# Linear attention with a ternary feed-forward layer: a matmul stage moved beside the next group's, and hi parts ahead of lo parts

## The reference

```python
def feature_map(x, orf):
    proj = x @ orf.T / d_k ** 0.25
    norm = jnp.sum(x * x, axis=-1, keepdims=True) / (2.0 * math.sqrt(d_k))
    return (jnp.exp(proj - norm) + EPS) / math.sqrt(m)
q = feature_map(split(x @ Wq.T + bq), orf)
k = feature_map(split(x @ Wk.T + bk), orf)
v = split(x @ Wv.T + bv)
kv = jnp.einsum('nlm,nld->nmd', k, v)
ksum = jnp.sum(k, axis=1)
buf = jnp.concatenate([kv, ksum[..., None]], axis=-1)
out = jnp.einsum('nlm,nmd->nld', q, buf)
out = out[..., :-1] / out[..., -1:]
# heads joined again, then
x = _layernorm(x + (out @ Wo.T + bo))
x = _layernorm(x + x @ (ternary(weight) * scale).T)
```

## Time and profile before

| | |
|---|---|
| time, median of 3 runs | 1310.24 us (1308.63 to 1312.22) |
| the profiled execution | 1310.11 us, span 1308.2 us |
| mean granted TensorE clock | 0.998 |
| busy: TensorE, weight loads, VectorE | 98%, 74%, 72% of the span |
| busy: ScalarE, GpSimd | 54%, 39% |
| TensorE in the chain that ended last | 83% |
| HBM | 39.13 MB read, 16.78 MB written |

### The profile page before, as it was taken

One profiled execution on the slowest core, in us unless ns is written; L12 is line 12 of the kernel. 1 busy time (PEld: TensorE's weight loads), 2 busy tenths in 40 slices (PEclk: granted clock), 3 DMA queues, 4 the chain that ended last, 5 costly groups with the idle time before them and its releaser, 6 DMA issues.

```text
span 1308.2 us, 25147 instructions
## 1 busy us (share of the span) xinstructions
PE 1279.2 (98%) x8570; PEld 965.2 (74%) x8570; DVE 946.1 (72%) x1791; ACT 701.9 (54%) x1403; POOL 511.1 (39%) x1005
## 2 busy tenths in 40 slices
PE   9999999999999999999999999999999999999886
PEld 8767787777877678776787768876788767886655
DVE  7599765886668775787657786577765787657866
ACT  5556535564355743657336663367544665346634
POOL 1325433345333443325424344334453334433343
PEclk9999999999999999999999999999999999999999
DMA  7557314763145721567215762257602675036611
GB/s 237 146 129 217 94 46 111 177 176 91 57 123 145 207 67 55 131 152 193 61 57 129 182 165 67 61 136 200 161 33 70 154 202 140 33 95 140 165 33 65
DMA packets 94015, 160.37 MB, mean 123 GB/s; under 512 B 31168, under 2 KB 47680, under 8 KB 93376
## 3 DMA queue, kind: packets, MB, share of 16 engines
q1 hardware_dynamic: 67856, 139.78, 41.5%
q10 hardware_dynamic: 9648, 16.85, 3.4%
q0 software_dynamic: 16384, 2.13, 1.2%
HBM read 39.13 MB, written 16.78 MB: 43 GB/s over the span
## 4 chain that ended last, share of the span: by engine, by line
PE 83%; DVE 5%; ACT 3%; SPq 3%; DMA 3%; issue 2%; POOL 1%; ACTq 0%; POOLq 0%; DVEq 0%
PE ps L927 27%; PE ps L964 24%; PE ps L1025 8%; PE ps L950 4%; PE ps L996 4%; PE ps L952 4%; PE ps L951 4%; PE ps L983 4%; PE ps L1051 2%; DMA rows<-in_x_t 1%; SPq L519 1%; ACT features L671 1%; SPq L508 1%; DMA rows<-in_Wk_t 1%; DMA stacks<-norm_rows 1%
## 5 line engine op out<-in xcount | busy, mean ns | idle before, releaser
L671 ACT ACTIVATE features<-ps 128x512 f32<-128x512 f32 x512 | 278.3, 601 | 257.3 <-PE ps L927 197.5
L574 POOL DMA_DIRECT2D stacks<-norm_rows x512 | 251.4, 499 | 397.4 <-DVE norm_rows L852 173.7
L553 POOL TENSOR_SCALAR stats<-stats 128x1 f32<-128x1 f32 x128 | 36.4, 284 | 317.9 <-DVE stats L780 317.9
L927 PE MATMUL ps<-Wo_hi,stacks 128*128 128x512 f32 x448 | 150.5, 402 | 0.0
L645 ACT ACTIVATE values_then_attention<-ps 128x512 f32<-128x512 f32 x64 | 38.2, 597 | 197.3 <-PE ps L952 194.0
L793 DVE TENSOR_TENSOR den<-den,features 128x512 f32<-128x512 f32 x192 | 132.3, 689 | 13.8 <-ACT features L671 0.4
L927 PE MATMUL ps<-orf_key_a,stacks 128*128 128x256 f32 x512 | 131.7, 289 | 1.1 <-DMA stacks<-norm_rows 1.1
L1025 PE MATMUL ps<-features,kv_ksum 128*32 128x512 f32 x1024 | 123.1, 598 | 5.9 <-ACT features L671 4.6
L927 PE MATMUL ps<-orf_key_b,stacks 68*128 68x256 f32 x512 | 128.5, 283 | 0.0
L829 DVE SCALAR_TENSOR_TENSOR unit_lo<-ps,cols,unit_hi 128x512 fp32r<-128x512 f32 x128 | 94.3, 736 | 35.0 <-ACT squares L655 35.0
L927 PEld LDWEIGHTS ps<-orf_key_a,stacks 128*128 128x128 f32 x512 | 97.1, 190 | 26.9 <-issue 23.0
(11 more groups left out here) (136 smaller groups left out, 2726.6 us busy)
## 6 DMA issues: line engine op xcount, KB each, us to landing
stacks<-unit_hi SPq DMA_DIRECT2D x384, 128.0 KB, 2.4
stacks<-unit_lo SPq DMA_DIRECT2D x256, 128.0 KB, 3.2
stacks<-unit_hi SPq DMA_DIRECT2D x64, 256.0 KB, 3.8
rows<-in_x_t SPq DMA_DIRECT2D x56, 256.0 KB, 3.6
out<-rows ACTq DMA_DIRECT2D x56, 256.0 KB, 2.0
stacks<-norm_rows POOLq DMA_DIRECT2D x512, 4.0 KB, 2.7
rows<-in_x SPq DMA_DIRECT2D x32, 256.0 KB, 4.0
features<-in_x SPq DMA_DIRECT2D x32, 256.0 KB, 4.1
```

Of the source, the lines that this page charges most:

```text
L574: pool.dma_start(slot[row:row + 1, c:c + L].rearrange("o (t c) -> o t c", c=DH), NN[DH * h:DH * (h + 1), u % 2, part, :].bitcast(F32)).the ...
L671: nc.scalar.activation(FE[:, n % 8, :, 0:M], ps[:, :].rearrange("p (a m) -> p a m", a=HG), ACT.Exp, scale=C_EXP).then_inc(a_exp.sem, 1)
L927: last = mm(out, a, b, start=(n == 0), stop=(n == len(terms) - 1))
```

## The change

- In `unit_stages`, a pair of stages, GG of half 1 and the R of half 1, goes from a group's query unit into the next group's key unit, wherever `joined(b, g)` holds: groups 0 to 2 of the batches before the last, and group 0 of the last. GG stands there directly ahead of the four G stages, and R after the next pair of F.
- In the key units 2, 4 and 6 the second half of the projection (`p[0]`) stands first, and S, L and the next projection half come before the second pair of F. G comes after four F, no longer after six.
- In unit 5, S, L, R and Q come in another order.
- Unit 0's projection of the next batch, O, OK and FF do their products with hi parts of the activations first, and wait for the lo part only then.

```diff
+def joined(b, g):
+    return g < (NG - 1 if b + 1 < B else 1)
...
         else:
-            seq = f(0, 1) + p[0] + f(2, 3) + p[1] + s0 + l0 + f(4, 5) + q0 + half + p[2] + f(6, 7) + s1 + l1 + q1 + norm + lift + p[3]
+            deferred, turned = ([("GG", b, g - 1, 1)], [("R", b, g - 1, 1)]) if joined(b, g - 1) else ([], [])
+            seq = p[0] + f(0, 1) + s0 + l0 + p[1] + f(2, 3) + deferred + half + f(4, 5) + turned + q0 + p[2] + f(6, 7) + s1 + l1 + q1 + norm + lift + p[3]
...
             seq += kv + f(2, 3) + p[1] + [("KVT", b, g)] + s0 + l0 + f(4, 5) + p[2] + f(6, 7) + s1 + q0 + [("GG", b, g, 0)]
-            seq += l1 + p[3] + [("R", b, g, 0), ("GG", b, g, 1)] + q1 + norm + lift
+            seq += l1 + p[3] + [("R", b, g, 0)] + ([] if joined(b, g) else [("GG", b, g, 1), ("R", b, g, 1)]) + q1 + norm + lift
         else:
             seq += xt(0) + kv + f(2, 3) + p[1] + [("KVT", b, g)] + s0 + l0 + xt(1, 2) + f(4, 5) + xt(3)
-            seq += [("LX", b + 1, t) for t in range(4, TT) if b + 1 < B] + p[2] + [("GG", b, g, 0), ("R", b, g, 0)] + q0
-            seq += s1 + xt(4) + f(6, 7) + xt(5) + l1 + p[3] + xt(6, 7) + [("GG", b, g, 1)] + q1 + norm + lift
+            seq += [("LX", b + 1, t) for t in range(4, TT) if b + 1 < B] + p[2] + [("GG", b, g, 0)] + s1 + l1
+            seq += [("R", b, g, 0)] + q0 + xt(4) + f(6, 7) + xt(5) + p[3] + xt(6, 7) + q1 + norm + lift
             seq += [("LR", b, t) for t in range(4)]
-        seq += [("R", b, g, 1)] if b + 1 < B or u < NU - 3 else []
...
                 elif kind == "P":
-                    if u == 0 and part == 0:
+                    if u == 0 and part == 0 and b:
+                        pe.wait_ge(a_xhi.sem, a_xhi.nth(b, 4 * h + 4))
+                    elif u == 0 and part == int(b > 0):
                         pe.wait_ge(*x_split(b, 4 * h + 3))
...
+                    if b and u == 0:
+                        terms = [t for n, t in enumerate(terms) if n % 3 < 2] + terms[2::3]
...
                 elif kind == "OK":
-                    pe.wait_ge(v_glo.sem, v_glo.nth(0, groups.index(part) + 1))
+                    pe.wait_ge(a_ghi.sem, a_ghi.nth(0, groups.index(part) + 1))
                     mm(ps[:, :], a_hi, WH["o"][:, k, :], start=(k == 0), stop=False)
                     mm(ps[:, :], a_hi, WL["o"][:, k, :], start=False, stop=False)
+                    pe.wait_ge(v_glo.sem, v_glo.nth(0, groups.index(part) + 1))
                     last = mm(ps[:, :], a_lo, WH["o"][:, k, :], start=False, stop=(k == KT - 1))
```

More of the change, by code:

```diff
@@ L1028, in _ @@
                 elif kind == "O":
-                    pe.wait_ge(v_alo.sem, v_alo.nth(b, u + 1))
+                    pe.wait_ge(a_ahi.sem, a_ahi.nth(b, u + 1))
                     if b == 0 and u == 0:
@@ L1033, in _ @@
                     al = ST[:, 1, 1024 + D * (u % 2):1024 + D * (u % 2 + 1)]
-                    terms = [t for k in range(KT) for t in (
-                        (ah[:, P * k:P * (k + 1)], WH["o"][:, k, :]), (ah[:, P * k:P * (k + 1)], WL["o"][:, k, :]),
-                        (al[:, P * k:P * (k + 1)], WH["o"][:, k, :]))]
-                    products(ps[:, :], terms).then_inc(t_o.sem, 1)
+                    for n, (k, w) in enumerate((k, w) for k in range(KT) for w in (WH["o"], WL["o"])):
+                        mm(ps[:, :], ah[:, P * k:P * (k + 1)], w[:, k, :], start=(n == 0), stop=False)
+                    pe.wait_ge(v_alo.sem, v_alo.nth(b, u + 1))
+                    for k in range(KT):
+                        last = mm(ps[:, :], al[:, P * k:P * (k + 1)], WH["o"][:, k, :], start=False, stop=(k == KT - 1))
+                    last.then_inc(t_o.sem, 1)
                 elif kind == "OK":
@@ L1055, in _ @@
                         pe.wait_ge(s_tern, KT)
+                    hi, lo = turned_rows(b, u)
+                    pe.wait_ge(a_yhi.sem, a_yhi.nth(b, u + 1))
+                    for k in range(KT):
+                        mm(ps[:, :], hi[:, P * k:P * (k + 1)], WT3[:, k, :], start=(k == 0), stop=False)
                     pe.wait_ge(v_ylo.sem, v_ylo.nth(b, u + 1))
-                    hi, lo = turned_rows(b, u)
-                    terms = [(part[:, P * k:P * (k + 1)], WT3[:, k, :]) for k in range(KT) for part in (hi, lo)]
-                    products(ps[:, :], terms).then_inc(t_ff.sem, 1)
+                    for k in range(KT):
+                        last = mm(ps[:, :], lo[:, P * k:P * (k + 1)], WT3[:, k, :], start=False, stop=(k == KT - 1))
+                    last.then_inc(t_ff.sem, 1)
 def kernel(**inputs):
```

## The result

| | before | changed |
|---|---|---|
| time, median of 14 runs each | 1310.71 us (1308.27 to 1313.02) | 1313.4 us (1311.43 to 1318.62) |
| ratio | | 1.0027 [1.0016, 1.0038] |
| the profiled execution, its span | 1310.11 us, 1308.2 | 1314.04 us, 1312.1 |
| mean granted TensorE clock | 0.998 | 0.993 |

The change costs 2.7 us by the medians, under 0.3%; the interval of the ratio lies clear of 1. The forecast was 1308.0 us, a gain of about 2; its range ended at 1312.8, 0.6 us too low.

A forecast was written before the change was run, and what follows sets the result against it. TensorE, busy in 98% of the span, was taken as the bound. 1310.1 - 4.65 (joined stretches) + 2.6 (norm rows) + 0.4 (unit 6) - 0.5 (output products) = 1308.0 us, no change; range 1301.0 to 1312.8.

The forecast's parts named there:

- The stretch of quadrant products: GG joined to G in 22 places saves 0.31 us each; 4.65 us in the 15 of units 2 and 4.
- Rival C: Joining GG and G saves nothing, as their different shapes need the same 0.31 us between them: 1312.7 us, chance 0.08.
- The walk of VectorE to the norms: Batch 3: moved VectorE work makes unit 4's norms later, leaving 7.65 us to its F(0) where there were 9.30.
- What is needed in between: From norms to F(0) of unit 4, issue and landing of norm rows need 7.3 to 10.3 us, by batch.
- rival A: Norm rows land in time, within 3.5 us, if they fall behind the x loads: 1305.4 us, chance 0.28.
- The term of 2.6 us: Cost of F(0) of unit 4 waiting for norm rows in batches 1 to 3; bounds 0 and 7 us.
- place two: Unit 6 and the next batch's key projection, seven places: 8.5 us gained, 8.9 of new x_hi waits, net cost 0.4.
- The rule on queues: DMA engines take turns between queues packet by packet, so small transfers would not stand behind big ones.
- The clock: TensorE's granted clock is at the higher level, 2.4 GHz, throughout, so it cannot bring much; no term in the sum.
- Rival B: Tile 7 is there in time for unit 6, so place two's 8.9 us are not paid: 1299.1 us, chance 0.11.
- Place three: Hi parts first in O, OK and FF: OK's two waits at the end shorten, 0.5 us saved, bounds 0 and 0.9.
- Rival D: VectorE becomes the bound of the key units, delaying norm rows: slower, 1314.6 us from a 1.1 us delay, chance 0.10.

The follow-up runs named there:

- experiment 9: Changed kernel with the deferred GG ahead of F 2 and 3, so not joined to G: 1326.7 us, ratio 1.0122 to the kernel before.
- Experiment 7: Changed kernel with the next batch's four x loads issued in unit 3 instead of unit 2: 1306.8 us, ratio 0.9967 to the kernel before.
- experiment 8: Kernel before the change with only its four x loads moved from unit 2 to unit 3: 1310.9 us, ratio 1.0001.
- experiment 1: Changed kernel with R of the deferred half moved behind the norms in the key units: 1310.5 us, ratio 0.9994 to the kernel before.
- Experiments 13 and 14: Kernel with the edits of experiments 1, 5 and 7 (1297.9 us), GpSimd writing 95 and 142 unread columns ahead of unit 4's norm rows: 1302.8 and 1319.3 us.
- Experiment 2: Changed kernel with units 5 and 6 back in the old order, GG joined in 15 places, not 22: 1314.8 us, ratio 1.0024 to the kernel before.
- experiments 5 and 6: 5: changed kernel, tile 7 and its projection half later in unit 6, 1311.1 us; 6: that plus R behind the norms, 1302.1 us.
- experiment 3: Kernel before the change with only the products reordered, hi parts first, in the old schedule: 1311.2 us, ratio 1.0006.
- experiment 4: Changed kernel with only its schedule, the products in their old order without hi parts first: 1329.7 us, ratio 1.0158 to the kernel before.

## Why the prediction was wrong, and where it was right

**The forecast said no change beyond what a measurement can tell (0.3%), and the 0.27% measured (by the ratio) are that, but on the other side, and outside the range.** Point by point:

- *The stretch of quadrant products, 0.31 us each, 22 places.* Right. G follows GG in 0.43; unit 1 to 3 gained 2.6 us in seven batches where 2.2 were reckoned; apart (experiment 9) it costs 0.47 a place, of which 0.13 is G's wait for features. The Trainium skill's rule (TensorEngine Tiling (Array Packing), Key Properties: a change of mode drains, one of tile does not) holds for the mixed pair as well. Rival C falls.
- *The walk of VectorE to the norms.* Right. It gave norms at 3.5 us behind F(0) of unit 3 (2.4 in the trace before, 0.77 later against an F(0) that is 0.31 earlier); the trace has 3.6. Of the 7.65 us to F(0) of unit 4, 7.5 are there where TensorE doesn't wait.
- *What is needed in between.* **This is the step that failed.** I took issue and landing from the trace before, batch by batch, and answered rival A with "the loads wait for the same VectorE run and shift with it". They don't: against F(0) of unit 3 the rows moved back by 1.2 us and the loads not at all (in batch 1 they came 0.7 sooner), and the rows slid in among them. Needed were 8.3 us in batch 4 and 9.2 in batch 5, where I had counted these two among those that wait for nothing; they wait 0.8 and 1.7. In batches 3 and 1 the 0.5 and 0.3 are what was reckoned (0.55, 0.35), in batch 2 nearly so (3.05 for 2.75); for batch 1 that is luck, since its need in the trace before was 7.4 us and not between 7.3 and 8.1. The term of 2.6 us measured 5.2 as waiting (6.3 less the 1.1 of before), twice its size and inside its bounds of 0 to 7. Of the 6.1 us that the row is off, 2.6 are this and 2.7 the low clock in batch 2 (below); most of the 0.8 left is what the five waits cost beyond their idle time, 0.14 us each. Unit 6, whose rows I had left out, waits 2.7 in all (see place two). Experiment 7 takes the loads away and gets 6.6 us back, experiment 8 gets nothing from them in the old kernel. It takes both, late rows and loads beside them: experiment 1 leaves the loads, issues the rows 1.5 us sooner, and of these waits only that of batch 2 is left.
- *Rival A* has it the wrong way round: rows that fall behind the loads were to land within 3.5 us, and took up to 5.2. Its 1305.4 is 1.1 too high by its own terms, since the 2.6 is already less the 1.1 of today. The rule on queues that it names stands in the section given at experiment 7.
- *The clock.* **It is the second thing that the sum had wrong, by leaving it out.** "Nor can the clock bring much" was carried over from the kernel before to one that pauses longer. The clock wasn't at the higher level throughout there either: behind the 2.4 us pause of batch 7 a stretch at 0.50 stands in its trace, within the mean of 0.998. The 2.7 us behind batch 2's pause have no term in the sum. Experiments 13 and 14 show that such stretches are made by pauses, and that a pause of one length brings one or not. That goes with the spread of the runs, 7.2 us in the changed kernel and 4.8 before: the slow ones have the low mean clock.
- *Place two, +0.4.* Near in sum (the trace has -0.7), but its own terms make another: 4.6 and 2.5 us of waits and 7 x 0.31 are 9.3 gained, not 8.5, and so a gain of 0.4. The waits there, 5.4 us on `x_hi` and 2.7 on norm rows, are 8.1 against 8.9 reckoned for `x_hi` alone: a unit that has waited for its rows comes later to tile 7. Experiment 2 finds nothing against it. That load wait was no law, though: experiments 5 and 6 remove it by giving TensorE and ScalarE other work first. Rival B asked only whether the tile would come in time by itself.
- *Place three, -0.5.* Nothing to be seen (experiment 3). That the same edit carries the new schedule (experiment 4) I had not priced apart.
- *Rival D* had the right sign, and one of its signs, waits on `stacks` in six or more units, came true. Its mechanism did not: VectorE was as late as reckoned and no later, the transfers were later. That the time came out 1.2 us from its 1314.6 is luck; the cause is one that the forecast had named and dismissed in one sentence.

Open stays how the DMA engines share their time between the loads and the rows; why batch 2, whose GpSimd queue pauses 1.7 us between two rows, waits longest in unit 4 in every kernel that waits there; what beside its length decides whether a pause brings a low clock; and why the x load lands later in experiment 1.

## What to carry to other kernels

When a producer is moved later on one queue, list what other queues do in the stretch that it moves into: a transfer's landing time was measured beside its old neighbours. An edit's gain at one place can be lost at the next (5.9 us gained and 4.2 lost in experiment 1, 5.0 and 2.8 in experiment 5), and another edit can keep it: 2.9 and 2.3 us alone, 11.3 together. So read gain and loss place by place, and try the pair before giving either up. And put a price on a pause of TensorE beyond its length, with a chance: in the last run 1.6 us more in three cases of seven, and in the changed kernel 2.7 behind its longest.

## What was unexpected of the hardware

- The granted clock stood at 0.50 to 0.61 behind some pauses of 1.7 to 3.1 us and at 1.00 behind others of 1.6 to 2.6 us at the same place. Under it 128x512 products start 0.42 us apart, not 0.23.
- The granted clock can fall when TensorE is busy again: behind the pause that ends at 735.9 (experiment 14) it falls 0.5 us later, with TensorE busy throughout the window from 736 on.
- In batch 5 eight 4 KB transfers land in at most 2.8 us without four 256 KB loads, and in up to 5.2 with them, though they are issued from another queue.
- Small MEMSETs on GpSimd that the trace shows with 0.10 us each start 0.034 us apart: 48 of them take 1.6 us, not 4.8.
